# Mixture-of-experts block: separate semaphores and reloads for an expert's two weights, and slots scaled in two halves

## The reference

```
h   = layernorm(x) * (1 + ca) + sa
x   = x + ga * attention(h)                     # 16 heads of 16, rope, causal softmax
h   = layernorm(x) * (1 + cb) + sb
xn  = rmsnorm(h, norm_gamma);  sn = rmsnorm(slot_embeds, slot_norm_gamma)
logits   = einsum('bnd,esd->bnes', xn, sn)      # 8 experts of 128 slots
dispatch = softmax(logits, over tokens);  combine = softmax(logits, over all 1024 slots)
slots = einsum('bnd,bnes->besd', xn, dispatch)
h  = gelu(slots @ w1[e] + b1[e])                # 256 -> 1024
eo = h @ w2[e] + b2[e]                          # 1024 -> 256
x  = x + gb * einsum('bmd,bnm->bnd', eo, combine)
```

## Time and profile before

| what | us |
|---|---|
| median of 3 runs (lowest, highest) | 3445.84 (3437.77, 3449.76) |
| profiled execution | 3442.23 |
| its span, first to last instruction | 3440.4 |
| TensorE busy | 3124.5 (91% of the span) |
| VectorE busy | 2216.7 (64%) |
| ScalarE busy | 1859.3 (54%) |
| mean granted TensorE clock | 0.967 of full speed |

### The profile page before, as it was taken

One profiled execution on the slowest core, in us unless ns is written; L12 is line 12 of the kernel. 1 busy time (PEld: TensorE's weight loads), 2 busy tenths in 40 slices (PEclk: granted clock), 3 DMA queues, 4 the chain that ended last, 5 costly groups with the idle time before them and its releaser, 6 DMA issues.

```text
span 3440.4 us, 45221 instructions
## 1 busy us (share of the span) xinstructions
PE 3124.5 (91%) x17500; PEld 1537.2 (45%) x17679; DVE 2216.7 (64%) x4245; ACT 1859.3 (54%) x3425; POOL 282.9 (8%) x155
## 2 busy tenths in 40 slices
PE   5799999998899999898989999988997999998899
PEld 3433332547553333353754333334575333334468
DVE  5878785562677788366367788836536877882632
ACT  2366667564236666745415666665541566666560
POOL 3100000110400000011130000002022000001200
PEclk9799999999999999999999999999999999999999
DMA  5222200015411120002432202010443221101042
GB/s 144 74 39 39 39 1 26 25 65 185 131 37 32 27 39 2 25 25 102 169 115 51 39 2 39 1 44 7 135 165 99 38 39 16 23 2 49 3 161 94
DMA packets 123554, 201.88 MB, mean 59 GB/s; under 512 B 10094, under 2 KB 106996, under 8 KB 120232
## 3 DMA queue, kind: packets, MB, share of 16 engines
q1 hardware_dynamic: 110820, 148.58, 13.4%
q10 hardware_dynamic: 12520, 50.40, 7.8%
HBM read 156.01 MB, written 42.16 MB: 58 GB/s over the span
## 4 chain that ended last, share of the span: by engine, by line
PE 69%; DVE 12%; ACT 8%; DMA 3%; issue 3%; POOL 2%; ACTq 1%; SPq 1%; DVEq 0%
PE ps L661 14%; PE ps L641 11%; PE ps L581 9%; PE ps L796 7%; DVE pm L1217 6%; PE ps L594 6%; PE ps L766 4%; ACT R L931 3%; PE ps L812 2%; DMA R<-in_L_ffn_w_dram 2%; PE ps L541 2%; PE ps L822 2%; PE ps L573 2%; PE ps L626 2%; PE ps L753 1%
## 5 line engine op out<-in xcount | busy, mean ns | idle before, releaser
L1217 DVE TENSOR_REDUCE pm<-ps 128x1 f32<-128x512 f32 (+4 forms) x2560 | 1395.4, 603 | 268.8 <-PE ps L581 191.9
L931 ACT ACTIVATE R<-ps 128x512 f32<-128x512 f32 (+1 forms) x2240 | 1190.4, 588 | 614.4 <-PE ps L641 421.6
L641 PE MATMUL ps<-R 99*128 99x512 bf16 (+3 forms) x2560 | 822.7, 354 | 27.0 <-ACT R L931 17.2
L661 PE MATMUL ps<-R 128*17 128x512 f32 (+3 forms) x5120 | 599.3, 542 | 27.5 <-ACT R L920 23.6
L581 PE MATMUL ps<-R 96*128 96x512 bf16 x1536 | 574.8, 385 | 24.9 <-DVE pm L1217 21.9
L641 PEld LDWEIGHTS ps<-R 99*128 99x128 bf16 x2560 | 237.8, 98 | 251.8 <-ACT R L931 140.7
L581 PEld LDWEIGHTS ps<-R 96*128 96x128 bf16 x1536 | 147.1, 97 | 453.5 <-DVE pm L1217 346.5
L796 PE MATMUL ps<-R 128*128 128x512 f32 x512 | 233.5, 615 | 12.5 <-ACT R L1029 12.5
L594 PE MATMUL ps<-R 128*128 128x257 f32 x1024 | 236.7, 387 | 4.1 <-ACT R L879 3.6
L766 PE MATMUL ps<-snT,R 128*128 128x512 f32 x512 | 234.2, 603 | 4.6 <-ACT R L969 4.6
L594 PEld LDWEIGHTS ps<-R 128*128 128x128 f32 x1024 | 197.3, 194 | 41.8 <-issue 12.1
(11 more groups left out here) (154 smaller groups left out, 3285.0 us busy)
## 6 DMA issues: line engine op xcount, KB each, us to landing
R<-in_L_ffn_w_dram SPq DMA_DIRECT2D x64, 1024.0 KB, 6.7
R<-q_parts ACTq DMA_DIRECT2D x12, 768.0 KB
R<-k_parts ACTq DMA_DIRECT2D x12, 768.0 KB
R<-in_L_attn_x_dram SPq DMA_DIRECT2D x16, 512.0 KB, 7.9
q_parts<-R SPq DMA_DIRECT2D x16, 512.0 KB, 3.8
k_parts<-R SPq DMA_DIRECT2D x16, 512.0 KB, 3.4
R<-in_L_attn_x_dram SPq DMA_DIRECT2D x4, 2048.0 KB, 8.3
x_park<-R SPq DMA_DIRECT2D x16, 512.0 KB, 2.6
```

What stands on the lines that cost most here:

```text
L641: last = mm(bank[:, i * w:(i + 1) * w], kst[g % 2][0:BROWS, h0 + i, j * P:(j + 1) * P], qst[g % 2][0:BROWS, h0 + i, (c + 1) * CH - w:(c + ...
L661: last = mm(ps[32 * h:32 * h + VC, 6, CH - w:CH], vall[:, j, HG * g + h, :], Eb[s % ESLOTS][:, h, 0:w], start=j == 0, stop=True, skip_grou ...
L931: A(Eb[s % ESLOTS][:, h0:h0 + n, 0:w], ps[:, u % NST, 0:n * w].rearrange("p (n w) -> p n w", n=n), ACT.Exp, scale=SCALE).then_inc(s_ex, 1)
L1217: mx = lambda o, i: V.tensor_reduce(o, i, AX.X, ALU.max)
```

## The change

`s_ew` becomes `s_ew1` for `w1` and `s_ew2` for `w2`; `hidden(e)` waits for the first, `expert_out(e)` for the second. SyncE's reload of `w1` for expert e waits for h(e-3) instead of y(e-3); that of `w2` still waits for y(e-3). In the last slot tile the two matmuls of slot half 0 come first and count up a new semaphore, `s_slh`; VectorE takes the banks of half 0 first; TensorE starts h0 after two of the four operations, and h1 after all four. So that h0 and h1 don't write banks that VectorE still has to read, even experts use banks 6 and 7 and odd ones 0 and 1 (`HIDDEN_BANK`).

```diff
--- before.py
+++ after.py
@@ -140,6 +140,7 @@
 ESLOTS = 4
 
 QU = 2 * NC
+HIDDEN_BANK = [6, 0]
 
 PROJ_BANK = [2, 3, 4, 5, 2, 3, 2, 3]
 PROJ_BEFORE = [None, None, None, None, 0, 1, 4, 5]
@@ -361,8 +362,10 @@
         s_edg = sem("dispatch_shifted_pool")
         s_ed = sem("dispatch_exponentials_ready")
         s_sl = sem("dispatch_tile_used")
+        s_slh = sem("first_slots_in_psum")
         s_sT = sem("slots_ready")
-        s_ew = [sem(f"expert_weights_loaded{i}") for i in range(NR)]
+        s_ew1 = [sem(f"first_weights_loaded{i}") for i in range(NR)]
+        s_ew2 = [sem(f"second_weights_loaded{i}") for i in range(NR)]
         s_b2 = sem("b2_loaded")
         s_h = sem("hidden_in_psum")
         s_g = sem("gelu_ready")
@@ -464,19 +467,24 @@
                     sp.dma_start(x1_park[b, :, 1024 * c:1024 * c + 1024],
                                  xres[:, 4 * c:4 * c + 4, :].rearrange("p t d -> p (t d)")).then_inc(s_park[c], 16)
 
-                def load_expert(e):
-                    sp.dma_start(w1s[e % NR], w1[e].rearrange("(k p) h -> p k h", p=P)).then_inc(s_ew[e % NR], 16)
-                    sp.dma_start(w2s[e % NR], w2[e].rearrange("(j p) d -> p j d", p=P)).then_inc(s_ew[e % NR], 16)
+                def load_first(e):
+                    sp.dma_start(w1s[e % NR], w1[e].rearrange("(k p) h -> p k h", p=P)).then_inc(s_ew1[e % NR], 16)
+
+                def load_second(e):
+                    sp.dma_start(w2s[e % NR], w2[e].rearrange("(j p) d -> p j d", p=P)).then_inc(s_ew2[e % NR], 16)
                 for e in range(NR):
                     sp.wait_ge(s_sl, b * 16 + 4 * (e + 1))
-                    load_expert(e)
+                    load_first(e)
+                    load_second(e)
                 sp.wait_ge(s_sl, b * 16 + 16)
                 sp.dma_start(b2b, b2.rearrange("(o e) d -> o e d", o=1).to_broadcast([P, E, D])).then_inc(s_b2, 16)
                 if b + 1 < B:
                     load_x(b + 1)
                 for e in range(NR, E):
+                    sp.wait_ge(s_h, b * 8 + e - NR + 1)
+                    load_first(e)
                     sp.wait_ge(s_y, b * 8 + e - NR + 1)
-                    load_expert(e)
+                    load_second(e)
                 sp.wait_ge(s_eo, b * 8 + 8)
                 for c in range(NC):
                     sp.wait_ge(s_park[c], (b + 1) * 16)
@@ -791,30 +799,36 @@
                     if n % 4 == 0:
                         pe.wait_ge(s_xn, b * 4 + n // 4 + 1)
                     pe.wait_ge(s_ed, b * 16 + n + 1)
-                    for k in range(KD):
-                        for mh in range(2):
-                            last = mm(ps[:, 2 * k + mh, :], xn[:, n, k * P:(k + 1) * P], L[:, n, mh * 512:(mh + 1) * 512],
-                                      start=n == 0, stop=n == NT - 1)
+                    for i in range(4):
+
+                        k, mh = (i % 2, i // 2) if n == NT - 1 else (i // 2, i % 2)
+                        last = mm(ps[:, 2 * k + mh, :], xn[:, n, k * P:(k + 1) * P], L[:, n, mh * 512:(mh + 1) * 512],
+                                  start=n == 0, stop=n == NT - 1)
+                        if n == NT - 1 and i == 1:
+                            last.then_inc(s_slh, 1)
                     last.then_inc(s_sl, 1)
                     if 1 <= n <= 4:
                         broadcast(n + 1)
                 broadcast(6)
                 broadcast(7)
 
-                pe.wait_ge(s_sT, b * 4 + 4)
+                pe.wait_ge(s_sT, b * 4 + 2)
 
                 def hidden(e):
-                    pe.wait_ge(s_ew[e % NR], b * 32 * len(range(e % NR, E, NR)) + 32 * (e // NR + 1))
+                    pe.wait_ge(s_ew1[e % NR], b * 16 * len(range(e % NR, E, NR)) + 16 * (e // NR + 1))
+                    if e == 1:
+                        pe.wait_ge(s_sT, b * 4 + 4)
                     if e >= 2:
                         pe.wait_ge(s_g, b * 8 + e - 1)
                     for j in range(JH):
                         for k in range(KD):
-                            last = mm(ps[:, 2 * (e % 2) + j // 4, (j % 4) * P:(j % 4 + 1) * P],
+                            last = mm(ps[:, HIDDEN_BANK[e % 2] + j // 4, (j % 4) * P:(j % 4 + 1) * P],
                                       w1s[e % NR][:, k, j * P:(j + 1) * P], slotsT[:, k, e * P:(e + 1) * P],
                                       start=k == 0, stop=k == 1)
                     last.then_inc(s_h, 1)
 
                 def expert_out(e):
+                    pe.wait_ge(s_ew2[e % NR], b * 16 * len(range(e % NR, E, NR)) + 16 * (e // NR + 1))
                     pe.wait_ge(s_g, b * 8 + e + 1)
                     if e >= 2:
                         pe.wait_ge(s_eo, b * 8 + e - 1)
@@ -1053,7 +1067,7 @@
                     if e >= 2:
                         act.wait_ge(s_y, b * 8 + e - 1)
                     for j in range(JH):
-                        last = A(hTe[e % 2][:, j, :], ps[:, 2 * (e % 2) + j // 4, (j % 4) * P:(j % 4 + 1) * P], ACT.Gelu,
+                        last = A(hTe[e % 2][:, j, :], ps[:, HIDDEN_BANK[e % 2] + j // 4, (j % 4) * P:(j % 4 + 1) * P], ACT.Gelu,
                                  bias=b1T[:, e * JH + j:e * JH + j + 1])
                     last.then_inc(s_g, 1)
                     if e == 3:
@@ -1398,9 +1412,11 @@
                 build_diag(dsum[:, 4:8], 7)
 
                 dve.wait_ge(s_be, b * 8 + 8)
-                dve.wait_ge(s_sl, b * 16 + 16)
-                for k in range(KD):
-                    for mh in range(2):
+                dve.wait_ge(s_slh, b + 1)
+                for mh in range(2):
+                    if mh:
+                        dve.wait_ge(s_sl, b * 16 + 16)
+                    for k in range(KD):
                         V.scalar_tensor_tensor(out=slotsT[:, k, mh * 512:(mh + 1) * 512], in0=ps[:, 2 * k + mh, :],
                                                scalar=gamcol[:, k:k + 1], in1=rdb[:, mh * 512:(mh + 1) * 512],
                                                op0=ALU.mult, op1=ALU.mult).then_inc(s_sT, 1)
```

## The result

| | before | changed |
|---|---|---|
| median, us (lowest, highest; runs) | 3447.8 (3437.8, 3457.1; 4) | 3425.8 (3424.7, 3426.6; 4) |
| ratio | | 0.9936, 95% interval 0.9908 to 0.9965 |
| profiled execution: span, mean clock | 3440.4, 0.967 | 3424.5, 0.968 |

What follows compares the result with a forecast made beforehand. TensorE, busy 91% of the span, was taken as the bound. Terms 4.9 + 4.8 + 8.0 + 0.7 - 2.5 = 15.9 us gave 3426.3 (profiled) and 3429.9 (median): forecast 3428, range 3421 to 3434, with rivals 3417 to 3438.

Steps and rivals of the forecast that it cites:

- first slots, y0 sooner: Before h0 in each batch: h0 waits for two slot operations, not four, so y0 comes sooner; 4.9 us won.
- weights, ahead of y2: h3's wait for the weights' transfers goes, one in each of four batches, with its restart; 4.8 us won.
- weights, y2 to y4: ScalarE already bounds this segment, so nothing is won except 0.7 us in batch 3, which has no square root.
- weights, y4 to y6: From y4 on, six waits for the weights' transfers go, with their restarts; 8.0 us won.
- clock behind the new pause: TensorE's new pause before y4 lowers the clock one time in two, three batches, 1.7 us each; 2.5 us lost.
- rival 1: The clock stays up in the pauses before h0 and y4; 21.3 us won, 3421 to 3424.5 us; chance 12%.
- ScalarE's bound for y0: ScalarE's exponentials, table load and Gelus keep y0 from starting before 10.69 us after the first slot operation.
- Rival 2: Weights' transfers share the engines and stay late; only the slots' 4.9 us is won, 3437.3 to 3441; chance 12%.
- The room of 14.2 us: Two pairs y, h between the issue of `w1` for experts 4 to 7 and its use, against 8.0 for both transfers.
- The pause before y4: TensorE stands still 1.9 us in one piece before y4, waiting for ScalarE, in the three batches with the square root.
- Rival 3: Long low-clock stretches behind the pauses before y4 and y0 lose 21.7 us against 18.4 won; 3449 on the median; 3%.

Runs made afterwards that it cites:

- weights only: Kernel before, with separate semaphores for `w1` and `w2` and `w1` reloaded after h(e-3), slots as before: 3442.9 us, ratio 0.9982.
- split only: Kernel before, with separate semaphores for `w1` and `w2`, both still reloaded after y(e-3): 3438.5 us, ratio 0.9976.
- early only: Kernel before, with `w1` reloaded after h(e-3) and one semaphore still counting both weights: 3438.7 us, ratio 0.9962.
- The run with the exponentials ahead: Changed kernel, with all eight combine exponentials moved ahead of ScalarE's copies of the last two broadcasts: 3421.0 us, second timing 3419.6.
- the last experiment: Changed kernel, with VectorE starting slot half 0 after broadcast 6's copy alone, exponentials not moved: 3438.4 us, second timing 3435.1.

## Why the prediction was right
Step by step, from the profiled executions before and after:

| step | predicted | measured |
|---|---|---|
| first slots, y0 sooner | 4.9 (3.8 to 7.8) | 7.4 |
| weights, ahead of y2 | 4.8 | 5.3 |
| weights, y2 to y4 | 0.7, batch 3 alone | 0.5 |
| weights, y4 to y6 | 8.0 | 8.6 |
| clock behind the new pause | -2.5 (-9.3 to 0) | 0 |
| sum | 15.9 | 21.8 |

So the mechanism was right at each step, and two sizes were off, the slots' part and the clock's price. The measured sum of 21.8 is nearer to rival 1's 21.3 than to the forecast's 15.9, although the clock did fall behind the pause before h0.

- *The first slots.* h0 1.33 us sooner: measured 1.32 (2.78 to 1.46 after the first slot operation). ScalarE's bound for y0: 10.69 predicted, 10.80 found. The size was off because I let the clock be as it was. It isn't: behind the 3.44 us pause the low clock lasted 6.8 us in 13 of 16 cases (four batches each of before, weights only, split only, early only) and 3.4 in the others; behind the 2.12 us pause it lasted 3.4 us in 24 of 24. Of the 2.2 us by which y0 comes sooner in batch 1, 0.9 is this. That the new semaphore for half 0 brings nothing by itself was argued from the releaser in the earlier trace rows and not tried alone.
- *The weights.* All 14 waits went, and what was late next is what was named: the segment from y2 to y4 did not move in three batches, since the Gelus of expert 4 hang on ScalarE's exponentials. The run with the exponentials ahead shows it: the same segment at 14.05 us. Rival 2 (the transfers share the engines and stay late) fell, even with one semaphore or with the late issue. The room of 14.2 us that I put against it was more than was needed: issued together with `w2`, `w1` lands within 6.4 us. Nothing was given back behind y7: from there to the next batch's values are 119.2 to 119.5 us, against 119.8 to 120.6 before.
- *The pause before y4*: 1.9 predicted, 1.98 found. Its price was mis-sized. Half of the 1.98 us pauses in the attention stage had lowered the clock, and I took one in two; in the expert stretch it was 3 of 24 (three batches each of eight profiles), and none in the changed kernel's own profile. At 1.7 us each that is 0.6 us for an execution, not 2.5.
- *Rival 1* (the clock stays up in both pauses) was right about the pause before y4 and wrong about that before h0, where it fell in every case. The rule of the Trainium skill, "TensorE: Matmul & The Clock Gate", under "Why this matters for your kernels", looks at the length of the gap alone, and would leave the clock up behind both. The trace doesn't agree: two gaps of nearly one length, 2.12 and 1.98 us, differ by 24 of 24 against 3 of 24. What TensorE did just before differs: before h0 it had run one broadcast of 1.1 us behind another pause of 0.79, before y4 two whole pairs. That this is what decides was not tried by itself.
- *Rival 3* (slower) did not occur here, but its mechanism is what made the last experiment slow: there a pause of 3.8 us at y0 lowered the clock in 7 of 8 batches.

The forecast of 3428 came from the sum on the profiled execution, 3426.3, and on the median, 3429.9; measured 3425.8. That these lie so close is in part luck: the sum was 6 us short of the 21.8 of the steps, and part of that was made up by starting from the profiled execution, which lay 3.6 us under the median. The span of the profiled execution fell by just the predicted 15.9 us, which is chance: the expert stretches fell by 21 to 22, and the attention stage of batch 0, which the change doesn't touch, was 6.8 us longer (from the first values to the first transposes of its output 492.3 against 485.5).

What stays open is the size beyond the stretch. The changed kernel was 22.0, 33.6 and 25.7 us under the kernel before on three occasions, with the same stretch to within 0.7 us; and the weights' part alone, in its three forms, was 7.2 to 11.6 us faster where the stretch says 12.4 to 14.1. The profiles show where the rest lies. From y7 to the next batch's first slots, three batches together:

| kernel | us | of these at clock 0.50 |
|---|---|---|
| before | 2128.9 | 118.6 |
| changed, three profiles | 2123.4 to 2126.7 | 90.5 to 100.4 |
| weights only, split only, early only | 2137.1, 2140.2, 2133.0 | 142.4, 148.8, 127.8 |

So in the weights' three forms these stages took 4 to 11 us longer than before and in the changed kernel 2.2 to 5.5 us less, and the time at the low clock goes the same way. Up to the first slots of batch 0 the changed kernel's three profiles differ among themselves, 717.7 to 730.3 us. Each row but the second has one profile for each kernel, and how an edit in the expert stretch comes to move the clock in stages that it doesn't touch, or whether it does, was not tested.

## What to carry to other kernels
When two resources are bound together by one semaphore, look whether the consumer needs both: splitting it or starting one transfer earlier each removed all the waits here, and doing both brought nothing more. Before shortening a wait, write down which engine is ready next and by how much; two of the segments here were ScalarE's already, and moving its work into a gap where it stood idle opened them. And count a pause of TensorE with the low clock behind it: here the pause before h0, moved to y0, where ScalarE set its end, became longer (3.84 us) and cost 10 us on the second occasion.

## What was not expected of the hardware
- The length of the low clock behind a pause depended on the pause: 3.44 us gave 6.8 us of it in 13 of 16, 2.12 us gave 3.4 us in 24 of 24, 0.21 us none in 12 of 12.
- Pauses of 2.12 and 1.98 us, with different work ahead of them, were followed by the low clock in 24 of 24 and 3 of 24 cases.
- The profile names "issue" for a wait whose releaser it doesn't find: the same pause before y4 has ScalarE as its releaser where the instruction waits only for ScalarE and VectorE, and "issue" where it also waits for `w2`, which in batch 0 had landed some 12 us before. At y0, which waits for `w2` too, the profile names ScalarE all the same, so "issue" doesn't mean that no engine is behind the wait.
